# Node weight matmuls of a graph kernel moved: W1 before the first hop, W2 into the last hop's finish

## What is computed

```python
def _hypergraph_conv(x, node_idx, edge_idx, D_inv, B_inv, W, b):
    xt = x @ W
    e = B_inv[:, None] * segment_sum(xt[node_idx], edge_idx)
    out = D_inv[:, None] * segment_sum(e[edge_idx], node_idx)
    return out + b

h = relu(layernorm(x))
h = relu(_hypergraph_conv(h, src, dst, D_inv, B_inv, W1, b1))
x = x + _hypergraph_conv(h, src, dst, D_inv, B_inv, W2, b2)
h = relu(layernorm(x))
x = x + edge_mlp_and_node_mlp(h, src, dst, edge_weight, ...)
```

## Time and profile before

| | us |
|---|---|
| median of 3 runs | 8347.98 |
| lowest and highest run | 8292.96, 8357.12 |
| the profiled execution's own time | 8329.03 |
| its span, first to last instruction | 8327.0 |
| TensorE busy | 7609.5 (91%) |
| VectorE busy | 7068.4 (85%) |
| ScalarE busy | 5286.8 (63%) |
| GpSimd busy | 3205.9 (38%) |

### The profile page before, as it was taken

One profiled execution on the slowest core, in us unless ns is written; L12 is line 12 of the kernel. 1 busy time (PEld: TensorE's weight loads), 2 busy tenths in 40 slices (PEclk: granted clock), 3 DMA queues, 4 the chain that ended last, 5 costly groups with the idle time before them and its releaser, 6 DMA issues. The chain is left out here.

```text
span 8327.0 us, 251689 instructions
## 1 busy us (share of the span) xinstructions
PE 7609.5 (91%) x80310; PEld 7121.8 (86%) x80310; DVE 7068.4 (85%) x15142; ACT 5286.8 (63%) x12950; POOL 3205.9 (38%) x4182
## 2 busy tenths in 40 slices
PE   1999999999999979999788899958999999999996
PEld 1888888888888879999788888858999999999994
DVE  7999999999999967775898888648999999999993
ACT  2899899898999940000677788625666666666662
POOL 4999999999999930000000000001111111111110
PEclk9999999999999989998999999859999999999998
DMA  2778777777777786664899999644333434333432
GB/s 68 160 175 173 170 175 171 173 173 168 177 171 173 173 194 190 191 190 122 197 222 223 216 245 246 164 126 129 116 116 115 116 114 117 113 117 113 116 115 70
DMA packets 1523000, 1309.63 MB, mean 157 GB/s; under 512 B 797344, under 2 KB 1337364, under 8 KB 1521212
## 3 DMA queue, kind: packets, MB, share of 16 engines
q1 hardware_dynamic: 1506126, 1269.86, 62.5%
q0 software_dynamic: 14112, 26.84, 1.2%
q10 hardware_dynamic: 1840, 0.53, 0.0%
HBM read 777.89 MB, written 361.62 MB: 137 GB/s over the span
## 5 line engine op out<-in xcount | busy, mean ns | idle before, releaser
L675 POOL TENSOR_SCALAR OH<-iot,kd 128x102 bf16<-128x102 bf16 x3440 | 2624.1, 781 | 0.0
L2270 POOL DMA_INDIRECT Qx<-tab_q,tidx x294 | 354.3, 1205 | 4680.5 <-DVE skt L2304 2582.3
L980 ACT ACTIVATE RB<-PS 128x512 uint8<-128x512 f32 x2401 | 1409.1, 601 | 117.8 <-PE PS L840 83.5
L1491 PE MATMUL wp<-AF,XS 128*128 128x256 f32 x9604 | 1194.6, 283 | 166.2 <-issue 130.8
L856 PE MATMUL HP<-T3a,RB 128*128 128x193 bf16 x9604 | 1213.3, 250 | 128.9 <-ACT RB L980 128.7
L1491 PEld LDWEIGHTS wp<-AF,XS 128*128 128x128 f32 x9604 | 1146.1, 190 | 197.6 <-issue 197.4
L1517 ACT ACTIVATE AF<-RG 128x1536 fp32r<-128x1536 uint8 x686 | 1022.6, 1491 | 329.1 <-PE wp L1491 216.9
L2291 ACT ACTIVATE Z<-Zb 128x512 f32<-128x512 f32 x882 | 556.0, 630 | 977.5 <-DVE Zb L2348 977.5
L856 PEld LDWEIGHTS HP<-T3a,RB 128*128 128x128 fp8e4 x9604 | 867.3, 98 | 215.4 <-issue 157.7
L2241 PEld LDWEIGHTS p<-eW2s,Y 128*128 128x128 f32 x7056 | 923.8, 191 | 23.9
L1571 DVE CAST AF<-RG 128x2048 fp32r<-128x2048 uint8 x686 | 811.9, 1222 | 143.4 <-DMA RG<-adjT 49.7
(11 more groups left out here) (340 smaller groups left out, 15054.1 us busy)
## 6 DMA issues: line engine op xcount, KB each, us to landing
RG<-adjT SPq DMA_DIRECT2D x1372, 224.0 KB, 6.7
sdb<-bk SPq DMA_DIRECT2D x245, 768.0 KB
adj<-RB SPq DMA_DIRECT2D x343, 448.0 KB, 2.9
adjT<-RT SPq DMA_DIRECT2D x686, 224.0 KB, 3.7
RG<-adj SPq DMA_DIRECT2D x686, 224.0 KB, 4.6
sdb<-bk SPq DMA_DIRECT2D x49, 384.0 KB
WR<-wk SPq DMA_DIRECT2D x882, 9.0 KB
tab_p<-Pst SPq DMA_DIRECT2D x25, 512.0 KB, 3.0
```

The source lines that it names most:

```text
L675: ins = e.tensor_scalar(OH[:, g * GT + k, :], iot1[:, 0:KEYS], kd[:, g * GT + k:g * GT + k + 1], None, ALU.is_equal)
L980: e.activation(RB[n % NSLOT][:, k, :].bitcast(u8).rearrange("p (n x) -> p n x", x=2), bank(u)[:, :].rearrange("p (x n) -> p n x", x=2), AC ...
L1491: ins = e.matmul(ps[b][:, 0:256], lhsT=XS[:, n * PB + m, :, :].rearrange("p c f -> p (c f)"), rhs=AF[:, (b + n) % 3, m, :], start=n == 0 a ...
```

## The change

- W1 is applied in the prologue: `X0` is transposed and multiplied group by group (`lin.tensor`), and the three bf16 parts of `T3a` are made from the sums in PSUM, by ScalarE (two copies a group) and VectorE (two subtractions a group, `split`, one group behind each `link`). GpSimd no longer takes part in this. The 136 increments now stand behind the matmuls in TensorE's stream.
- The first hop's finish adds b1, makes relu and writes `XS1` itself (four more VectorE instructions a chunk). Linear a and the block behind it are gone.
- In the last hop `fold` is replaced by W2 stacked twice (`W22`), so that the turn is the product with W2. The nodes' own part must therefore enter ahead of it: VectorE makes a diagonal `DGw` and a copy `XO` (`selves`), and TensorE adds two matmuls of 128 columns a turn. The finish has two VectorE instructions in place of four.
- Linear b is gone; a block copies `H3` to `acc64`. Only three blocks of `X` are cleared, and the addition to x stands behind the preparation of the found keys.

```diff
+            rs = [sbt(st, f"rs{n}", [P, GB, F], fp32) for n in range(2)]
+            lin.buffers(st, "w")
...
-                    v = X0[:, 0:BLK, :]
+                    for g in range(NG + 2):
+                        if g < NG:
+                            e.wait_ge(lin.turned, g + 1)
+                            if g >= 2:
+                                e.wait_ge(lin.made, g - 1)
+                            e.activation(lin.hT[g % 2][:, :, :].rearrange("p j n -> p (j n)"), lin.pt[g % 2][0:F, :], ACT.Copy).then_inc(lin.copied, 1)
+                        if 1 <= g <= NG:
+                            e.wait_ge(lin.made, g)
+                            e.activation(third(g - 1, 0), turned_sums(g - 1), ACT.Copy).then_inc(u_0, 1)
+                        if g >= 2:
+                            e.wait_ge(lin.out, g - 1)
+                            e.activation(third(g - 2, 1), held(rs[g % 2], g - 2), ACT.Copy).then_inc(u_1, 1)
+
+                @block.tensor
+                def _(e):
                     e.wait_ge(norm.steps, 8)
...
+                    lin.tensor(e, 0, X0, nW["W1s"])
                     spaced(e, SPACE1)
...
+                    def split(g):
+
+                        if g < NG:
+                            e.wait_ge(u_0, g + 1)
+                            past(e, u_r, g - 1)
+                            e.tensor_tensor(held(rs[g % 2], g), turned_sums(g), third(g, 0), ALU.subtract).then_inc(lin.out, 1)
+                        if g >= 1:
+                            e.wait_ge(u_1, g)
+                            e.tensor_tensor(third(g - 1, 2), held(rs[(g - 1) % 2], g - 1), third(g - 1, 1), ALU.subtract).then_inc(u_r, 1)
...
                         ins.then_inc(s_c, 1)
+                        if at < NG:
+                            split(at)
+                            at += 1
                         e.wait_ge(s_c, n)
...
-                    for n in range(2):
-                        v, a = X0[:, 0:BLK, :], n * F
-                        e.wait_ge(l_s, 2 * n + 2)
-                        e.tensor_tensor(v, v, T3a[:, :, a:a + F], ALU.subtract).then_inc(l_s, 1)
...
-                                    did(e.tensor_tensor(H2[:, DS(c * 2, 2), :], et[:, :, :], q, ALU.mult), i)
+                                    did(e.tensor_tensor(et[:, :, :], et[:, :, :], q, ALU.mult), i)
+                                    did(e.tensor_tensor(et[:, :, :], et[:, :, :], nW["b1s"][:, :].unsqueeze(1).to_broadcast([P, 2, F]), ALU.add), i)
+                                    did(e.tensor_scalar(et[:, :, :], et[:, :, :], 0.0, None, ALU.max), i)
+                                    hi, lo = (XS1[:, DS(c * 2, 2), n, :] for n in range(2))
+                                    did(e.tensor_copy(hi, et[:, :, :]), i)
+                                    did(e.tensor_tensor(lo, et[:, :, :], hi, ALU.subtract), i)
...
+                                        if n == 3 and r == 2:
+                                            for h in range(2):
+                                                e.matmul(ps[b][:, h * P:(h + 1) * P], lhsT=XO[b][:, h, :], rhs=DGw[b][:, h, :],
+                                                         start=False, stop=False, skip_group_check=True)
...
+                                    if r == 2:
+                                        e.wait_ge(h_z, c + (by + 1))
+                                        did(e.tensor_tensor(et[:, :, :], sums, each(cinv[k]), ALU.mult))
+                                        e.sem_inc(h_d, 1)
+                                        did(e.tensor_tensor(to[:, DS(c * 2, 2), :], et[:, :, :], nW["b2s"][:, :].unsqueeze(1).to_broadcast([P, 2, F]), ALU.add))
+                                        return
...
+                                def selves(i, b):
+
+                                    own = selfc[:, DS(i * 2, 2)].unsqueeze(2).to_broadcast([P, 2, P])
+                                    e.scalar_tensor_tensor(DGw[b][:, :, :], idn[:, :].unsqueeze(1).to_broadcast([P, 2, P]), 1.0 / TWO, own, ALU.mult, ALU.mult)
+                                    e.tensor_copy(XO[b][:, :, :].rearrange("p h (c f) -> p h c f", f=F), XS[:, DS(i * 2, 2), :, :])
...
+                                        if n == 2 and r == 2:
+                                            selves(i, b)
...
-                linear("a", H2, nW["W1s"], add_bias("b1s"))
...
-                wide_hop(2, backward, XS2, "s", H3)
...
-                linear("b", H3, nW["W2s"], add_bias("b2s"))
...
+                wide_hop(2, backward, XS2, "s", H3, sbt(x1, "AF2", [P, 3, PB, 256], f32r), W22)
...
+                        e.tensor_copy(acc64, H3[:, :, :]).then_inc(l_s, 1)
+                        e.wait_ge(l_s, 2)
...
+                    e.memset(X[:, 97:NB, :], 0.0).then_inc(l_s, 1)
                     e.memset(WB[:, :], 0.0)
-                    e.memset(X[:, :, :], 0.0).then_inc(l_s, 1)
...
-                    e.wait_ge(l_x, 64)
-                    e.tensor_tensor(X[:, :, :], X[:, :, :], acc64, ALU.add).then_inc(l_s, 1)
-                    e.wait_ge(l_s, 17)
...
                     step(e.tensor_scalar(xov[:, 0:1], found[0][:, NX:NX + 1], 0.0, None, ALU.is_gt))
+                    e.wait_ge(l_x, 64)
+                    e.tensor_tensor(X[:, :, :], X[:, :, :], acc64, ALU.add).then_inc(l_s, 1)
+                    e.wait_ge(l_s, 9)
```

More of the change, by code:

```diff
@@ L241, in gnn_kernel @@
             loads.append((nW[name][:, :], a))
+        W22 = sbt(root, "W22", [P, F], fp32)
+        for n in range(2):
+            loads.append((W22[n * F:(n + 1) * F, :], W2))
         for name, a, n in (("b1s", b1, F), ("b2s", b2, F), ("nb2s", nb2, F), ("eb2s", eb2, HID),
@@ L334, in gnn_kernel @@
         l_x, l_s = sem("l_x"), sem("l_s")
+        u_0, u_r, u_1, u_2, u_q = (sem(f"u_{n}") for n in ("0", "r", "1", "2", "q"))
         norm = Norm("a")
@@ L353, in gnn_kernel, with third, held, turned_sums @@
             bad = sbt(st, "bad", [P, 1], fp32)
+            rs = [sbt(st, f"rs{n}", [P, GB, F], fp32) for n in range(2)]
+            lin.buffers(st, "w")
+            calls[0] += 1
+            def third(g, c):
+                return T3a[:, g * GB:min((g + 1) * GB, BLK), c * F:(c + 1) * F]
+            def held(t, g):
+                return t[:, 0:min(GB, BLK - g * GB), :]
+            def turned_sums(g):
+                return held(lin.po[g % 2][:, 0:GB * F].rearrange("p (j n) -> p j n", n=F), g)
             with nc.Block() as block:
@@ L359, in _ @@
                     norm.scalar(e)
-                    v = X0[:, 0:BLK, :]
[L361 to L366, removed]
+                    for g in range(NG + 2):
[10 more added lines that the diff above has]
+                            e.activation(third(g - 2, 1), held(rs[g % 2], g - 2), ACT.Copy).then_inc(u_1, 1)
                 @block.tensor
                 def _(e):
+                    e.wait_ge(norm.steps, 8)
+                    e.wait_ge(s_w, 16 * len(loads))
+                    e.wait_ge(s_fill, 3)
+                    lin.tensor(e, 0, X0, nW["W1s"])
                     spaced(e, SPACE1)
@@ L438, in _ @@
                     link(e.tensor_tensor(cum[:, :], cum[:, :], part[:, :], ALU.add))
+                    for g in range(at, NG + 1):
+                        split(g)
                 @block.gpsimd
@@ L1252, in gnn_kernel @@
                 keyed2 = sbt(hx, "keyed2", [P, RECS], fp32)
-                h0 = hx.enter_context(ExitStack())
-                H2 = sbt(h0, "H2", [P, NB, F], fp32)
+                DGw = [sbt(hx, f"DGw{n}", [P, 2, P], f32r) for n in range(3)]
+                XO = [sbt(hx, f"XO{n}", [P, 2, 2 * F], f32r) for n in range(3)]
+                x1 = hx.enter_context(ExitStack())
+                XS1 = sbt(x1, "XS1", [P, BLK, 2, F], f32r)
+                h0 = x1.enter_context(ExitStack())
                 zero = sbt(h0, "zeroh", [P, 2 * W3], bf16)
@@ L1261, in gnn_kernel @@
                 recs = sbt(h0, "recs", [P, RECS, 2], fp32)
-                keyed = [sbt(h0, f"keyed{n}", [P, RECS], fp32) for n in range(2)] + [keyed2]
+                keyed = [ACC[:, BLK * W3 // 2:BLK * W3 // 2 + RECS], sbt(h0, "keyed1", [P, RECS], fp32), keyed2]
                 h_l = [sem(f"h_l{n}") for n in range(NPC)]
@@ L1587, in gnn_kernel @@
                 first_hop(backward, T3bf, "s")
-                linear("a", H2, nW["W1s"], add_bias("b1s"))
                 h0.close()
-                AF = sbt(hx, "AF", [P, 3, PB, 256], f32r)
-                x1 = hx.enter_context(ExitStack())
-                XS1 = sbt(x1, "XS1", [P, BLK, 2, F], f32r)
+                accx.close()
+                XS2 = right("XS2", [P, BLK, 2, F], f32r)
+                af = ExitStack()
+                wide_hop(1, forward, XS1, "d", XS2, sbt(af, "AF1", [P, 3, PB, 256], f32r), fold)
+                af.close()
+                x1.close()
+                H3 = sbt(x1, "H3", [P, NB, F], fp32)
+                wide_hop(2, backward, XS2, "s", H3, sbt(x1, "AF2", [P, 3, PB, 256], f32r), W22)
```

(2 more changed lines are left out.)

57 lines of the change are left out of this document (19 added, 38 removed).

## The result

The changed kernel takes 8301.70 us (median of five runs), against 8349.60 for the kernel before (median of five). One of the five, at 10,730.72 us with a granted clock of 0.655, ran in a slower state of the chip; the other four lie between 8258.91 and 8305.85, with a median of 8296.72. The ratio from those four is 0.9937, with an interval of 0.9909 to 0.9964. The gain is 48 us by the medians of five (53 by the four) where 145 were forecast, and the time lies above the range. It is also less than the 1% (83 us) that the prediction held to be tellable; the interval excludes 1 all the same. The profiled execution took 8301.70 us with a span of 8299.9, against a span of 8327.0 before: 27 us less.

The account below looks back on a forecast made before the run. Long stages were bound by engines or transfers the change hardly touches, with linear a and b bare on the path. Terms -85.2, -83.4, +21 (prologue) and +3 (last hop) gave -145: 8348 to 8203 us, range 8150 to 8265.

Parts of the forecast that it names:

- the term of nothing for the edge stage: Edge stage: no change in length was forecast, 0 us.
- the third rival: Stage 1 and edge loops, moved against code packets, may stall every lap; slower from 3.0 us a lap; chance 0.08.
- The increments: Prologue: TensorE's 136 increments, now behind the last matmul, add 3.8 us, bounds 0 to +10.
- The prologue's walk: Prologue: group-by-group chain of linear a ends at 152.0 against VectorE's 134.70 before, +17.3 us.
- Key steps beside no GpSimd subtraction: Prologue: without GpSimd's subtractions, L413 and L416 fall from 13.23 to 1.84 us, returning 22.8 us to VectorE.
- both removals: Between stages: removing linear a with the relu block gains 85.2 us, removing linear b 83.4 us.
- the first hop: First hop: four added VectorE instructions a chunk, 1.3 to 1.7 us, stay hidden under its 2.59 us wait.
- The two matmuls a turn: Last hop: two added 128-column matmuls a turn at 0.23 us each take 22 us of TensorE time, mostly covered.
- the last hop: Last hop: shorter finish, added `selves` steps and matmuls together cost +3 us, bounds -5 and +35.
- rival 1: Last hop: TensorE or VectorE becomes its bound, +35 us, kernel at 8235 us; chance 0.14.
- rival 2: Prologue: it runs at the upper clock or overlaps better, kernel at 8190 us; chance 0.06.
- rival 4: First hop: added steps cost 3.1 instead of 1.5 and do not hide, 25 us, kernel at 8228; chance 0.04.

Follow-up runs that it names:

- run 8: Changed kernel with 256 more increments ahead of the edge stage (370 in place of 114): 8334.09 us, edge stage 2549.3 us.
- run 9: Kernel before with 72 increments added on VectorE alone: 8344.40 us, stage 1 2934.9 us.
- run 4: Changed kernel with the 136 increments moved ahead of the prologue's matmuls, number unchanged: 8273.83 us.
- run 3: Changed kernel with 24 in place of 136 increments behind the prologue's matmuls and 226 in place of 114 ahead of the edge stage: 8302.52 us.
- run 11: run 5 plus 184 increments on VectorE and 160 on ScalarE, all four loops at old places modulo 256: 8175.63 us, ratio 0.9798.
- run 10: Kernel before with 97 increments added on ScalarE alone, behind its weight loads: 8296.51 us.
- run 7: Kernel before with 72 increments added on VectorE and 97 on ScalarE: 8351.70 us, stage 1 2938.9 us.
- run 2: Kernel before with 28 in place of 114 increments ahead of the edge stage: 8432.87 us, ratio 1.0082.
- run 5: run 4 with 24 increments ahead of the prologue's matmuls and 56 ahead of the edge stage: 8200.24 us, ratio 0.9813.

## Why the prediction was wrong, step by step

**The failed step is the term of nothing for the edge stage.** The sum held code delivery at zero and left it to the third rival, which I gave 0.08 ("that a lap waits for it, no row shows"). It was the largest single loss: 79.0 us in the edge stage, 79.0 / 22 = 3.6 us for each jump taken (I had counted 24 laps). The rival had the mechanism and its place (no slack in the edge stage, so paid in full). Its prices were for both loops: 3.0 us a lap in each would have used up the whole gain, and here one loop alone paid. My argument against it, "no such idle time stands in the stages now", spoke of the kernel before, whose loops stood well; it could not speak for the changed one. And `spaced` itself, 250 instructions that do nothing but shift the stream, was in the code that I read: I treated it as a cost of 3.8 us instead of asking what moving it undoes. The measured sum differs from the forecast one by 118 us: 79.0 here, 25.9 in stage 1, 8.1 in the prologue, and 5 in small terms. The Trainium skill, page "Runtime: NRT & Kernel Launch", section "Instruction fetch mechanics", says that instructions come in blocks of 256 and that a taken branch out of the fetched window waits for a fetch; run 8, in which a move by 256 left the edge stage as long as it was, agrees with that block, and the jump's own record (0.45 us before, 3.4 after) with that wait. What decides between a good and a bad place within it, no run shows: two places of TensorE's edge loop were tried, 70 and 240. Nor was the other lever tried: both kernels announce each of these jumps with a hint in TensorE's stream (`BRANCH_PREFETCH_HINT` in the trace), 8.5 us ahead of it in both, and no run moved the hint.

**In stage 1** I had looked at TensorE's stream only. Its stall came (29.0 us) and was hidden, as that rival had it. VectorE's stream, which the change lengthens too, was not in the prediction at all, and by run 9 it cost 21.5 of the 25.9. Why GpSimd pays is open: it is the bound there, its one-hots have no more idle time ahead of them than before, but each is longer (a mean of 781 ns before, 787 with VectorE's loop moved: 20 us over 3440 of them). That they are slowed by VectorE's shifted work beside them would fit, and was not tested.

**The increments** were a mis-sized term. I priced 136 at 43 ns less a hidden part, 3.8 us, with 10 as the bound. One every 0.154 us makes 20.9, of which 17.0 were left on the path (run 4). From run 3 to run 8 the stretch ahead of the layer norm grew by 22.1 us for 144 more, the same 0.153 each. A mean over mixed matmul instructions was no bound for an instruction that updates a semaphore. The cost itself was removable for nothing, since at the head of the stream TensorE waits for the layer norm anyway.

**The prologue's walk** was right in kind and 4.7 us too long (147.3 for 152.0). Of these, 1.2 are arithmetic: 125.7 and eight groups of 2.885 give 148.8, where I wrote 150.0. The groups behind 3.5 us key steps came every 4.09 us (89.18 to 93.27), not 4.43: a long step takes 3.51 and two subtractions 0.66 between starts, less the overlap, where I had added full lengths. Key steps beside no GpSimd subtraction took 1.83 for 13.23, as predicted, and the group period at the end was 2.89.

**Right were** both removals (85.4 for 85.2, 82.8 for 83.4) and the first hop, where VectorE's wait fell from 2.6 to 1.3 and the length did not change. The two matmuls a turn measured 16.5 us of TensorE time for the 22 assumed. That the last hop came out at +3.4 for +3 is luck as far as these profiles go: from its first to its last matmul it took 642.7 us before and 645.9 after, but 639.2 to 656.8 in the six kernels that leave it as it was. The wide hop, whose code did not change, is 4.4 us longer in the ledger; by the same kind of cut it has 715.2 to 718.4 us in those six and 716.5 to 723.2 in the eight with the change. No run looked for the cause. Rivals 1, 2 and 4 did not happen. With the code back in place (run 11) the span is 8173.9, 153 below that of before, where the terms summed to 145; its prologue costs 10.9 us where 21 were forecast. The medians differ by more, 169, since the profiled execution of before (8329.03) lay 15 below the median beside run 11.

## What to carry to other kernels

When a change adds or removes instructions ahead of a loop that streams its code (instruction packets counted per lap, more than a few), the loop's place is part of the change: count the instructions on every engine, TensorE and VectorE alike, restore the place (modulo 256 was enough here), and only then judge the edit. A stall of one to three microseconds once a lap, booked as issue or as a wait for a step already done, is its sign, and the length of the closing jump's own record can show it directly. Filler belongs where its engine waits anyway, not behind its last useful instruction.

## What the runs showed of the hardware

**The same code ran at either clock level.** In run 10 linear b was done in half the time. First its timeline, then that of the kernel before, at the same instructions:

```profile
5362.29 0.63 PE L279 MATMUL ptb<-idn,H 128*64 128x128 f32 x4
5362.85 1.10 PE L287 MATMUL pob<-W2s,hTb 64*128 64x64 f32 x8
```

```profile
5374.75 1.06 PE L279 MATMUL ptb<-idn,H 128*64 128x128 f32 x4
5375.74 1.97 PE L287 MATMUL pob<-W2s,hTb 64*128 64x64 f32 x8
```

The granted clock of these stretches (busy time of run 10, then of before):

```profile
5365.00:5380.00 15.00, 15.00 (x115) 12.55 (x115) 3.94 (x10) 5.45 (x10) 0.00 (x0) 1.00 0.01 2
```

```profile
5365.00:5380.00 15.00, 15.00 (x65) 12.12 (x64) 2.12 (x5) 2.95 (x5) 0.00 (x0) 0.50 0.01 1
```

TensorE came out of the last hop at 1.00 in both. In the kernel before it fell within the first microseconds of linear b (0.56 over 5350 to 5365). In one execution it kept 2.4 GHz through linear b, in the other five profiles of such kernels it fell to 1.2, and that is worth 32 us (stretch to the layer norm 89.4, for 120.2 to 121.5 in the others). The ScalarE edit cannot be its cause alone, since run 7 contains it and has 121.3. What decides is not shown. Runs of the kernel before down to 8292.96 may be of the same kind; none of them was profiled.

**The clock column says nothing before its first record.** In the prologue of the changed kernel (66 to 145) it reads 1.00:

```profile
66.00:145.00 79.00, 68.55 (x286) 55.22 (x286) 60.58 (x72) 30.05 (x70) 0.00 (x0) 1.00 0.10 42
```

Yet four transposes take 1.06 us and eight matmuls 1.97 there, exactly as in linear b at 0.50. By durations the prologue ran at 1.2 GHz, as forecast, and the column does not show it.

**The output stage** took 190 to 193 us in most profiles and 207 in those of runs 2, 3 and 5. In run 3 its mean granted clock was 0.76, in run 11 (above) 0.81:

```profile
8094.00:8300.80 206.80, 139.09 (x804) 93.98 (x801) 62.76 (x122) 50.35 (x80) 0.00 (x0) 0.76 0.27 64
```

So 14 us of run 3's time, which hid the gain of its shorter prologue, belong to this and not to its edit.
